# Window attention in fp32: output projection with split operands, all row maxima subtracted on GpSimd, projected heads copied out of PSUM by ScalarE and the residual added in SBUF by GpSimd

## The reference

```
x = x + L0(group_norm(x))     # layer norm, linear recurrence over the 49 tokens of a 7x7 window, MLP
x = x + L1(group_norm(x))     # shifted window attention, 12 heads of 16 dimensions

def L1(x):                                     # windows of 7x7 = 49 tokens, shifted by 3
    qkv = windows(x) @ qkv_w.T + qkv_b
    q, k, v = qkv[0] * 16 ** -0.5, qkv[1], qkv[2]
    attn = softmax(q @ k.T + bias_of_head + shift_mask)
    out = (attn @ v) @ proj_w.T + proj_b       # the heads side by side: 192 -> 192
    return windows_back(out)
```

## Time and profile before

| | us |
|---|---|
| median of 3 executions | 4775.11 |
| lowest, highest | 4772.32, 4776.53 |
| the profiled execution | 4771.51 |
| its span, first to last instruction | 4769.7 |
| attention stage, by the start of its first transposes | about 2503 to the end |
| one unit, from one to the next | 17.57 |

### The profile page before, as it was taken

The page is one execution under the profiler, slowest core; times in us unless marked ns, Lnnn a source line. Parts: engine busy times, 40 slices in busy tenths (PEclk is TensorE's granted clock), DMA queues, the critical chain, the costliest instruction groups (busy, mean ns, idle before and its releaser), DMA issues. The chain is left out here.

```text
span 4769.7 us, 140614 instructions
## 1 busy us (share of the span) xinstructions
PE 4464.8 (94%) x51720; PEld 3768.6 (79%) x51720; DVE 4038.5 (85%) x7594; ACT 2472.6 (52%) x4850; POOL 2481.5 (52%) x2098
## 2 busy tenths in 40 slices
PE   0599999999999999999969999999999999999999
PEld 0488888888888888888857777777777777777777
DVE  6788888888888888888838888888888888888887
ACT  0244444444444444444416666666666666666665
POOL 1245555455545555455525555555555555555555
PEclk9999999999999999999969999999999999999999
DMA  8011111111111111111112222222222222222222
GB/s 341 21 38 38 39 39 41 37 39 39 41 37 38 39 39 40 37 39 39 37 40 66 71 67 70 67 70 68 68 71 66 71 67 70 69 68 70 67 71 59
DMA packets 389802, 286.01 MB, mean 60 GB/s; under 512 B 147164, under 2 KB 388044, under 8 KB 388556
## 3 DMA queue, kind: packets, MB, share of 16 engines
q1 hardware_dynamic: 387012, 283.15, 20.3%
q10 hardware_dynamic: 2736, 2.14, 0.1%
HBM read 120.34 MB, written 87.31 MB: 44 GB/s over the span
## 5 line engine op out<-in xcount | busy, mean ns | idle before, releaser
L887 POOL TENSOR_TENSOR E<-E,ri 128x588 f32<-128x588 f32 x512 | 601.5, 1175 | 410.4 <-DVE ri L1119 410.4
L893 POOL TENSOR_TENSOR L<-L,mx 128x294 f32<-128x294 f32 x512 | 483.4, 944 | 511.7 <-DVE mx L1105 511.7
L603 PE MATMUL ps_o<-w,g_hi 128*128 128x384 f32 x2352 | 710.6, 365 | 5.9 <-DVE g_lo L543 4.1
L415 ACT ACTIVATE gF<-ps_g,b1f 128x512 f32<-128x512 f32 x588 | 406.0, 691 | 394.0 <-PE ps_g L634 391.3
L976 ACT ACTIVATE PT<-ps_t 98x588 f32<-98x588 f32 x512 | 342.7, 669 | 461.4 <-PE ps_t L1253 451.3
L1101 DVE SCALAR_TENSOR_TENSOR L<-ps_s,bias 128x588 f32<-128x588 f32 x512 | 384.1, 750 | 230.8 <-PE ps_s L1170 230.8
L603 PE MATMUL ps_o<-w,g_lo 128*128 128x192 f32 x2352 | 534.9, 255 | 0.0
L1170 PE MATMUL ps_s<-Kp,Q 32*64 32x98 f32 x12288 | 494.0, 259 | 1.5 <-POOL E L887 0.6
L442 POOL TENSOR_TENSOR res<-xt,b2b 128x768 f32<-128x768 f32 x98 | 181.1, 1848 | 591.4 <-DVE x L491 591.4
L401 ACT ACTIVATE h_hi<-ps_h,hbias 128x512 fp32r<-128x512 f32 x196 | 123.2, 679 | 703.1 <-PE ps_h L618 703.1
L603 PEld LDWEIGHTS ps_o<-w,g_hi 128*128 128x128 f32 x2352 | 429.7, 189 | 27.1 <-issue 25.1
(11 more groups left out here) (211 smaller groups left out, 12030.9 us busy)
## 6 DMA issues: line engine op xcount, KB each, us to landing
xs<-in_x SPq DMA_DIRECT2D x8, 4704.0 KB, 22.5
xt<-in_x SPq DMA_DIRECT2D x98, 384.0 KB, 3.4
x_cells<-x SPq DMA_DIRECT2D x784, 48.0 KB
xb<-x_cells SPq DMA_DIRECT2D x128, 294.0 KB
Vx<-V SPq DMA_DIRECT2D x512, 73.5 KB
out<-yo SPq DMA_DIRECT2D x128, 294.0 KB
Kp<-K SPq DMA_DIRECT2D x256, 98.0 KB, 2.0
Kp<-K SPq DMA_DIRECT2D x256, 49.0 KB, 2.2
```

The costliest lines, as they stand in the source:

```text
L415: act.activation(gF[f % 4][:, :], ps_g[:, f % 2, :], ACT.Gelu, bias=b1f[:, f:f + 1]).then_inc(s_gelu, 1)
L603: last = pe.matmul(dst, g[:, f, P * k:P * (k + 1)], w, start=(f == 0 and i == 0), stop=(f == FT - 1 and i == 1))
L887: pool.tensor_tensor(e, e, ri[p][:, :].unsqueeze(2).to_broadcast([P, HEADS, T]), ALU.mult)\
L893: pool.tensor_tensor(l, l, mx[p][:, HS:HEADS].unsqueeze(2).to_broadcast([P, HEADS - HS, T]), ALU.subtract).then_inc(s_sbp, 1)
```

## The change

- **The output projection has split operands.** `wp` gets upper and lower parts (`W_P`), and so do the heads: ACT writes `o_hi` where it wrote `oT`, with the bias added, and DVE writes what is left over from `ps_v` (`heads_lower`, two instructions for each pair: 128x98 to `o_lo` and 64x98 into the spare half of `o_hi`). `mix` then takes ten fp32r matmuls for a half unit in place of four plain fp32 ones.
- **The maxima of all 12 heads are subtracted on GpSimd,** in one instruction of 128x588; DVE's half goes.
- **The projected heads are copied out of PSUM by ACT** (`projected`, two of 98x384 for each unit) and the residual is added in SBUF by GpSimd (`add_residual`, two of 98x384); DVE's `finish` goes.
- **What is moved:** `mix` of the first half goes from step 2 to step 1; `turn` stands behind the values product of step 0, both of DVE's `lower` behind the sums and reciprocals of step 0, `project(1)` goes from the end of step 1 to the middle of step 2, `project(0)` stands behind the values product of step 1. `values` of half 0 goes to step 3 and of half 1 to step 0 of the next slot, with ACT's copies of V; the `Vx` DMAs go to the head of SP's next slot. `rs` goes from step 0 to step 1 on GpSimd; the store is one slot later. The tasks of the three shared PSUM banks are dealt out anew.

```diff
-            TURN, KEYS, OUT0, QRY, VAL, OUT1 = 0, 2, 4, 5, 6, 8
+            VAL1, TURN, OUT0, KEYS, QRY, VAL0, OUT1 = 0, 1, 3, 4, 6, 7, 8
...
                 def less_max(u, p):
                     pool.wait_ge(s_mx, UP * u + p + 1)
-                    l = L[p][:, HS:HEADS, :]
-                    pool.tensor_tensor(l, l, mx[p][:, HS:HEADS].unsqueeze(2).to_broadcast([P, HEADS - HS, T]),
-                                       ALU.subtract).then_inc(s_sbp, 1)
+                    l = L[p][:, :, :]
+                    pool.tensor_tensor(l, l, mx[p][:, :].unsqueeze(2).to_broadcast([P, HEADS, T]),
+                                       ALU.subtract).then_inc(s_sub, 1)
+
+                def add_residual(u, c, half):
+                    pool.wait_ge(s_ye, 2 * u + half + 1)
+                    ab = slice(2 * half, 2 * half + 2)
+                    y = yo[c][0:T2, ab, :]
+                    pool.tensor_tensor(y, y, rs[c][0:T2, ab, :], ALU.add).then_inc(s_yo, 1)
...
-                        if is_unit(u) and p == 0:
+                        if is_unit(u - 2) and p == 0:
+                            add_residual(u - 2, c, 1)
+                        if is_unit(u - 1) and p == 2:
+                            add_residual(u - 1, 1 - c, 0)
+                        if is_unit(u) and p == 1:
...
+                def projected(i, c, half):
+                    v, d = 2 * i + c - 1, 1 - c
+                    act.wait_ge(s_pj, 2 * v + half + 1)
...
+                    full = ps_w(OUT1 if half else OUT0)[0:T2, 0:2 * C].rearrange("p (a c) -> p a c", a=2)
+                    act.activation(yo[d][0:T2, 2 * half:2 * half + 2, :], full, ACT.Copy).then_inc(s_ye, 1)
...
-                def finish(i, c, half):
...
-                    dve.tensor_tensor(yo[d][0:T2, ab, :], full, rs[d][0:T2, ab, :], ALU.add).then_inc(s_yo, 1)
+                def heads_lower(u, c, p):
+                    dve.wait_ge(s_oh, UP * u + p + 1)
+                    dve.scalar_tensor_tensor(out=o_lo[c][p][:, :], in0=ps_v[:, 0:T2], scalar=vb[c][:, 0:1],
+                                             in1=o_hi[c][p][:, 0, :], op0=ALU.add, op1=ALU.subtract)
+                    dve.scalar_tensor_tensor(out=o_hi[c][p][CB:P, 1, :], in0=ps_v[0:CB, T2:2 * T2],
+                                             scalar=vb[c][0:CB, 1:2], in1=o_hi[c][p][0:CB, 1, :],
+                                             op0=ALU.add, op1=ALU.subtract).then_inc(s_o, 1)
...
+                        if is_unit(u - 1):
+                            heads_lower(u - 1, 1 - c, p)
...
                     for a in range(2):
                         p = 2 * half + a
-                        for k in range(2):
-                            last = pe.matmul(ps_w(OUT1 if half else OUT0)[0:T2, C * a:C * (a + 1)],
-                                             oT[d][p][:, k, :], wp[:, k, :], start=(k == 0), stop=(k == 1))
+                        terms = W_P.terms(o_hi[d][p], o_lo[d][p], slice(0, C))
+                        for k, (w, o) in enumerate(terms):
+                            last = pe.matmul(ps_w(OUT1 if half else OUT0)[0:T2, C * a:C * (a + 1)], o, w,
+                                             start=(k == 0), stop=(k == len(terms) - 1))
```

More of the change, by code:

```diff
@@ L724, in build @@
             PT = [sb(f"PT{b}", [P, JP, T2]) for b in range(2)]
-            oT = [[sb(f"oT{b}{p}", [P, 2, T2]) for p in range(UP)] for b in range(2)]
+            o_hi = [[sb(f"o_hi{b}{p}", [P, 2, T2], f32r) for p in range(UP)] for b in range(2)]
+            o_lo = [[sb(f"o_lo{b}{p}", [P, T2], f32r) for p in range(UP)] for b in range(2)]
             ps_s = ps("ps_s", [P, 2, 512])
@@ L775, in build @@
             LOADS = 1 + 1
-            WEIGHT_LOADS3 = 5
+            WEIGHT_LOADS3 = 4
             K_SPREADS = 2 * HB
@@ L831, in slot @@
                     u = 2 * i + c
+                    if is_unit(u):
+                        for half in range(2):
+                            sp.wait_ge(s_vc[half], u + 1)
+                        for w in range(2):
+                            for e in range(2):
+                                sp.dma_start(Vx[c][T * e:T * (e + 1), w:NW:2, JP * HD * e:JP * HD * (e + 1)],
+                                             V[T * w:T * (w + 1), :, JP * HD * e:JP * HD * (e + 1)])\
+                                  .then_inc(s_vx[c], 16)
                     if is_unit(u + 2):
@@ L845, in slot @@
                                 sp.dma_start(Kp[d][rows, k, e, :, :], K[rows, k, :, :]).then_inc(s_kp[d], 16)
[L847 to L858, removed]
+                    if is_unit(u - 2):
+                        sp.wait_ge(s_yo, 2 * (u - 1))
+                        sp.dma_start(out[bass.ds(u - 2, 1), :, :, :, :].rearrange("u p w t c -> (u w t) p c"),
+                                     yo[c][0:T2, :, :]).then_inc(s_so[c], 16)
                 units(sp, slot)
@@ L922, in _ @@
                 act.wait_ge(s_w3, 16 * WEIGHT_LOADS3)
-                for t in range(2):
-                    last = act.activation(W_QKV.parts[2 * t][:, :], raw[:, t, :], ACT.Copy)
+                for full, parts in ((raw, W_QKV), (wp, W_P)):
+                    for t in range(2):
+                        last = act.activation(parts.parts[2 * t][:, :], full[:, t, :], ACT.Copy)
                 last.then_inc(s_ws3, 1)
@@ L1119, in slot @@
                             dve.reciprocal(ri[pp][:, :], sm[pp][:, :]).then_inc(s_ri, 1)
[L1120 to L1123 removed]
+                        if nxt and p == 0:
+                            lower(i, c, 0)
+                            lower(i, c, 1)
                 units(dve, slot)
```

139 lines of the change are left out of this document (59 added, 80 removed).

## The result

The changed kernel takes **4818.5 us** (median of 5 runs, 4814.62 to 4878.62) against 4775.07 (5 runs, 4772.32 to 4776.53) on the same chip: a ratio of 1.0121, with a 95% interval from 1.0096 to 1.0147. By the medians it is 43 us slower; the ratio is one of means, and the one long run of 4878.62 raises it. I had forecast 4728, with 4672 to 4792 as the range.

A forecast was written before the change was run, and what follows sets the result against it. PE was taken as the bound at 17.57 us a unit; -1.16 for `mix`, -0.67 old stall, +1.16 and +0.29 new waits gave about 17.20. Saving 0.37 in 128 units, 47 us, it forecast 4728 us, range 4672 to 4792.

The forecast's parts named there:

- both waits: PE waits 1.16 us at step 1's `mix` for the heads' lower parts, then 0.29 at the next scores for `Kp`.
- zero: Start of the unit's count: the end of the second scores of step 0; `mix` was forecast 4.88 us later.
- the landing of `Kp`: The last `Kp` DMA lands 2.0 us after its start, at least 1.9 and at most 2.4.
- the chain behind `rs`: After GpSimd's `rs`, SP issues the load, then four `Kp` DMAs; the keys land at 15.76 us.
- `mix` at -0.58 for each half: On PE, ten fp32r matmuls take 0.89 us instead of 1.47, twice a unit: -1.16 us.
- the moved steps issue the same matmuls as before: On PE, steps placed elsewhere keep the same matmuls, so no change in PE's time was counted for them.
- it comes out even: `heads_lower` at 0.42 makes the unit 17.40, or 0.2 more before `Kp` makes 17.6: 4765 to 4785 us; chance 0.11.
- The first (keys not late, 4691): `Kp` arrives in time, so PE's own road with its wait for the heads bounds: 16.91 us a unit; chance 0.20.
- The second (GpSimd twice as slow): GpSimd's 12-head subtraction takes about twice its six-head time, 1.9 us: 4824 us; chance of slower in all 0.12.
- The fourth (no waits, 4541 to 4626): PE is merely 1.16 us shorter, old stall gone or kept: 15.7 to 16.4 us a unit; chance 0.03.
- The fifth, that the split brings nothing: In `mix`, ten fp32r matmuls take as long as four fp32 ones; counted inside the 0.12 chance for slower.

The follow-up runs named there:

- the changed one's repeat: The changed kernel unaltered, run again beside its variant without the residual part, on the same chip: 4833.5 us, ratio 1.0127.
- The pair without waits: Changed kernel with `Kp` DMAs ahead of SP's load, plus plain fp32 `mix` (4702.04 us) or split `mix` and pair 1's `heads_lower` ahead of `lower` (4601.87 us).
- the regrouped kernel: Changed kernel with early `heads_lower`, `Kp` DMAs ahead of SP's load, and values product moved so fp32r groups adjoin: 4562.28 us, ratio 0.9555.
- The filled kernel: Changed kernel plus ten extra fp32r matmuls on PE ahead of the first `mix`'s wait for the heads, their sums overwritten: 4787.31 us, ratio 1.0029.
- keys first: Changed kernel with SP issuing the four `Kp` DMAs ahead of the load that waits for `rs`: 4789.68 us, ratio 1.0032.
- the two edits of one place each: Changed kernel with pair 1's `heads_lower` ahead of both `lower` and the `Kp` DMAs ahead of SP's load: 4601.87 us, ratio 0.9642.
- The kernel with plain operands: Changed kernel with ACT writing plain fp32 heads, `heads_lower` gone and `mix` in plain fp32 matmuls, order kept: 4711.51 us, ratio 0.9872.

## Why the prediction was wrong

**What held.** The kind: both waits are where I put them, in the order in which I put them. At full clock `mix` starts 4.90 us behind zero in one unit and 5.02 in the next (forecast 4.88). That it is so near is partly luck: `values` ahead of it took 1.08 and not 0.89, and DVE was done 4.85 behind zero and not 4.74, but PE followed 0.05 later and not 0.14. `heads_lower` takes 0.32 and 0.31 with its gaps, the wait 1.1 each (forecast 1.16), GpSimd's subtraction 1.175 at the median, the landing of `Kp` 2.05, the chain behind `rs` all there, if 0.3 late in sum. By the Trainium skill, "VectorE: DVE Perf Modes", section "The TRN2 errata — SBUF-src ops pay a fixed extra latency per instruction", `heads_lower` is an estimate of 0.23 us; the trace doesn't agree, with 0.32. The advice of the Trainium skill, "GPSIMD Engine Reference", section "Engine selection", to keep such work on VectorE did not pay in this order of work: with half of the maxima back on VectorE the kernel was 78 us slower than the changed one's repeat.

**The term that was mis-sized: the first one, `mix` at -0.58 for each half.** I took 0.89 us for ten fp32r matmuls from a `values` that stood directly behind a projection. The new places of `mix` are behind scores, transposes or a wait. The trace of before had the right row, one unit step later, and I passed over it:

```profile
3504.64 1.09 PE ps_w L1194 x5
...
3507.91 1.07 PE ps_w L1207 x10
```

That is `values` behind scores, at 1.07. In the changed kernel `mix` takes 1.14 and 1.05 to 1.07, so the saving is 0.33 + 0.40. And "the moved steps issue the same matmuls as before" was true of the count but not of the time: one half of `values` stood behind a projection at 0.89 and now stands behind scores at 1.08. Together 0.33 + 0.40 - 0.19 = **0.54 us for a unit, not 1.16**. The pair without waits, 4702.04 against 4601.87, gives 0.78 for the matmuls alone, in agreement with 1.47 - 1.07 = 0.40 twice; the regrouped kernel shows that the neighbour is the cause.

Put into the prediction's own sum: PE is ready for the next unit's scores at 16.13 and not at 15.57; the keys land at 16.08 and not at 15.76, and the scores start at 16.12 to 16.3. With 1.37 for the scores this is 17.5 to 17.7, not 17.20. So without the clock the change would have been even, or with the additional slot 11 us slower: near "it comes out even", my third rival, though by another cause than I gave it. (The filled kernel is 14 us slower than the kernel before on its chip.) Of the 90 us between forecast and result, 0.39 us for each of 128 units are 50 and the clock is 31; most of the rest is the longer end.

**The step that was missing: what a recurring wait does to the clock.** I counted the new wait at its length. Before, PE waited 0.67 us in each unit at a clock of 1.00; with 1.1 us the clock falls now and then, and part of PE's work behind the wait runs at 1.2 GHz. The filled kernel puts this at 31 us, and it is what makes the result slower rather than even. That the fall comes with this wait is shown by the removal of the wait (a mean clock of 0.980 to 0.989 in all runs of the six kernels in which `mix` waits little or not at all, 0.950 to 0.979 in all runs of those that keep it), and by the filled kernel, which keeps DVE's order and gives PE work in its place. Why some units fall and others with the same wait don't, and why the clock then stays down for a whole unit in which PE doesn't wait, is not shown by anything here.

**My rivals.** The first (keys not late, 4691) was wrong: the keys cost 0.2 us, as keys first showed. The second (GpSimd twice as slow) was wrong by its row, 1.175. (The six-head form took 0.957 at the median here too, with the maxima back on both engines, but 0.677 at the shortest; so it can be quicker than the row I doubled.) One reading behind it was loose: DVE's subtraction of 1.87 us ended at 3502.57, 0.32 after POOL's `rs`, and not with it. The fourth (no waits, 4541 to 4626) is not the changed kernel, but it is where the two edits of one place each lead: 4601.87. The fifth, that the split brings nothing, is wrong for the matmuls (of 0.58 for each half 0.40 were there) but near the outcome in this order of work: the wait for the lower parts, which only the split needs, cost more than that. The kernel with plain operands is 107 us faster.

## What to carry to other kernels

Price a group of matmuls by a row with the same *neighbour ahead of it*, not only with the same shapes, and price the groups that are moved as well as those that are changed. When a change shortens the bounding engine's work but hangs it on a longer road over other engines, look for both waits at once: removing either alone brought 29 or 80 us, removing both 217. And a wait of about a microsecond that recurs in each unit can cost more than its length, as here, when the granted clock falls behind it, so give the operand that is last an earlier place, or put work into the wait.

## What the runs showed of the hardware

- **A matmul group's neighbour.** Ten fp32r matmuls (98 columns of weights, 192 moving) take 1.07 us behind transposes, scores or a value product in plain fp32 and 0.89 behind another fp32r group; five of 392 moving columns 1.09 and 0.92. That is 0.17 to 0.18 us for each step from plain fp32 to fp32r; two projections in a row take 1.99, not 2.18.
- **The clock.** With one wait of 1.1 us in each unit of 17.6 the granted clock was 0.94 over 1900 us, and 0.50 in a whole unit in which PE didn't wait; with ten more matmuls in that wait it was 1.00, and the kernel 31 us faster. With a wait of 0.67 us it had been 1.00.
- **GpSimd.** An instruction with one operand spread out from 12 columns takes 1.175 us for 588 elements, one of two full operands 1.00 for 384 and 1.84 for 768: the spread operand is not the dearer one.
